# Attention on one core: maxima sent on ScalarE's queue, softmax sums inverted by way of DRAM and multiplied in on GpSimd

## What is computed

```
q_lat, kv_lat = h @ W_qd, h @ W_kvd          # h = rmsnorm(xn, w_ln1)
scores = einsum('bqhd,bkhd->bhqk', qq, kk) * scale      # 16 heads, 16 wide, causal
probs  = softmax(scores, axis=-1)
y      = einsum('bhqk,bkhd->bqhd', probs, v).reshape(B, S, H) @ W_o
x1     = xn + y
x2     = x1 + shared_expert(rmsnorm(x1)) + top2_of_7_experts(rmsnorm(x1))
```

## Time and profile before

| | |
|---|---|
| median of 3 runs | 4965.75 us |
| the profiled execution, its own time | 4929.39 us |
| its span | 4927.6 us |
| TensorE's mean granted clock in it | 0.889 of full speed |
| PE, VectorE, ScalarE, GpSimd busy | 79%, 68%, 48%, 44% of the span |

### The profile page before, as it was taken

One profiled execution on the slowest core, in us unless ns is written; L12 is line 12 of the kernel. 1 busy time (PEld: TensorE's weight loads), 2 busy tenths in 40 slices (PEclk: granted clock), 3 DMA queues, 4 the chain that ended last, 5 costly groups with the idle time before them and its releaser, 6 DMA issues.

```text
span 4927.6 us, 72057 instructions
## 1 busy us (share of the span) xinstructions
PE 3871.0 (79%) x22968; PEld 2870.5 (58%) x22968; DVE 3372.8 (68%) x5931; ACT 2389.0 (48%) x6217; POOL 2172.9 (44%) x1174
## 2 busy tenths in 40 slices
PE   3677777777777778599958888888888888888886
PEld 1333333334433344477747777777777777777776
DVE  2555555555555556222229999999999999999998
ACT  0322223222232333133337667767767767767764
POOL 3222222222222221100037777677677777777775
PEclk7888888888988989799978999999999999999998
DMA  4444434343433330476632212222222222122121
GB/s 70 64 66 66 65 61 67 58 66 61 66 61 61 63 59 31 122 211 211 210 99 76 76 71 80 78 73 76 78 73 78 75 79 80 68 82 77 71 76 41
DMA packets 285539, 399.85 MB, mean 81 GB/s; under 512 B 50773, under 2 KB 247766, under 8 KB 268824
## 3 DMA queue, kind: packets, MB, share of 16 engines
q1 hardware_dynamic: 272920, 362.63, 29.9%
q0 software_dynamic: 12288, 33.57, 2.0%
HBM read 313.26 MB, written 82.05 MB: 80 GB/s over the span
## 4 chain that ended last, share of the span: by engine, by line
DVE 19%; POOL 11%; PE 10%; issue 9%; DVEq 1%; ACT 1%; SPq 0%; POOLq 0%; DMA 0%; ACTq 0%
POOL m_ub L1505 9%; PE m_Y L1870 4%; DVE m_S L1723 4%; DVE m_S L1731 4%; DVE m_PR L1723 4%; DVE m_PR L1731 3%; PE m_Y L1880 3%; DVE m_sp_v L1700 2%; POOL m_yg L1515 1%; PE m_Y L1883 1%; DVE m_ub L1708 1%; POOL m_dtx L1484 1%; DVE m_yz L1742 1%; DVE m_st L1679 0%; PE m_F L1824 0%
## 5 line engine op out<-in xcount | busy, mean ns | idle before, releaser
L1505 POOL TENSOR_TENSOR m_ub<-m_Bb,m_dtx 128x2048 f32<-128x2048 f32 x256 | 1156.3, 4540 | 554.6 <-PE m_Y L1870 548.0
L1620 ACT ACTIVATE m_dA<-m_dt,m_a_neg 128x128 f32<-128x128 f32 x4096 | 1210.4, 392 | 29.6 <-DVE m_S L1731 25.6
L1870 PE MATMUL m_Y<-m_ub,m_ident 128*128 128x128 f32 x8192 | 1013.8, 288 | 240.2 <-DVE m_ub L1708 240.2
L1870 PEld LDWEIGHTS m_Y<-m_ub,m_ident 128*128 128x128 f32 x8192 | 995.3, 204 | 248.5 <-DVE m_ub L1708 247.7
L506 ACT ACTIVATE f_pt<-f_X 128x512 f32<-128x512 f32 (+1 forms) x704 | 378.4, 556 | 886.1 <-PE f_X L792 884.6
L559 DVE TENSOR_REDUCE f_nm<-f_Y 128x1 f32<-128x512 f32 (+3 forms) x896 | 430.3, 529 | 148.7 <-PE f_Y L786 147.0
L791 PE MATMUL f_X<-f_qst,f_kst 99*128 99x512 bf16 (+3 forms) x1024 | 300.1, 336 | 294.7 <-DMA f_qst<-f_nmT 213.0
L617 DVE RECIPROCAL f_O<-f_O 128x256 f32<-128x256 f32 x128 | 222.6, 1751 | 360.2 <-PE f_O L847 360.2
L1723 DVE SCALAR_TENSOR_TENSOR m_PR<-m_dA,m_S 128x512 f32<-128x512 f32 x512 | 355.5, 694 | 122.1 <-POOL m_ub L1505 50.0
L785 PE MATMUL f_Y<-f_kst,f_qst 96*128 96x512 bf16 (+3 forms) x1024 | 276.1, 324 | 161.1 <-DVE f_nm L559 128.2
L791 PEld LDWEIGHTS f_X<-f_qst,f_kst 99*128 99x128 bf16 x1024 | 108.9, 107 | 449.3 <-issue 310.0
(11 more groups left out here) (239 smaller groups left out, 6924.0 us busy)
## 6 DMA issues: line engine op xcount, KB each, us to landing
m_Bb<-m_bc_dram SPq DMA_DIRECT2D x64, 1024.0 KB, 4.7
m_Cb<-m_bc_dram SPq DMA_DIRECT2D x64, 1024.0 KB, 4.7
f_parts_dram<-f_parts SPq DMA_DIRECT2D x32, 768.0 KB, 4.5
f_kst<-f_parts_dram SPq DMA_DIRECT2D x192, 128.0 KB, 11.3
f_qst<-f_parts_dram SPq DMA_DIRECT2D x192, 128.0 KB, 12.3
e_rows<-sorted_rows SPq DMA_DIRECT2D x70, 256.0 KB, 2.7
e_wg<-Wg SPq DMA_DIRECT2D x70, 256.0 KB, 2.9
e_wu<-Wu SPq DMA_DIRECT2D x70, 256.0 KB, 3.9
```

The lines of the kernel that those rows point to most:

```text
L1505: pool.tensor_tensor(ub[:, h, i, :, :], Bb[:, s, :, :], dtx[:, par, m, None, s * SN:(s + 1) * SN].to_broadcast([P, NST, SN]), ALU.mult).th ...
L1620: last = act.activation(dA[:, h, i, n, :], dtt[:, par, m, s * SN:(s + 1) * SN], ACT.Exp, scale=a_neg[:, m, n:n + 1])
L1870: last = pe.matmul(Y[:, i * SN:(i + 1) * SN], ident[:, :], ub[:, h, i, n, :], start=False, stop=(n == NST - 1), skip_group_check=True)
```

## The change

The maxima are sent by ScalarE (`act.dma_start` in `nmt`) instead of SP. The sums are no longer spread by PE and inverted in full banks. For two groups at a time (a pair): `so` stores the four sum rows of both groups (4 partitions x 1024, 16 KB) to DRAM, `sl` loads them as a tile of 128x32, `rp` inverts that tile on VectorE, `ro` stores it, `rl` loads it back spread over 128 rows (128x1024, 512 KB, by a broadcast access pattern of 4 x 32 x 1024), and `ym` multiplies on GpSimd, 128x1024. All four are issued by ScalarE, and it waits before each of `so`, `sl`, `ro` and `rl` for what comes ahead. The second pair of a batch is finished in the next round (`sl1` to `ym1`). PE's wait before reusing a bank `f_O` is now for the copy. The second product of the shared expert is written over the first (`hm = sg`), and the table `AT` is new: 62 places rather than 74, `s1` over places 5 to 55 (before: 8 to 63), the group stores, `pfx`, `scat` and `nm` nearer to the round's end.

The diff (semaphores' declarations, the constant `f_sel` and line counts left out):

```diff
...
@@ -81,7 +80,11 @@
     rb = sb("f_rb", [P, 2, SEQ])
-    yT = sb("f_yT", [P, 4, SEQ])
+    yT = sb("f_yT", [P, NG, SEQ])
+    PAIRS = NG // 2
+    PW = HG * 2 * SEQ // P
+    sums = sb("f_sums", [P, PAIRS, PW])
+    shares = sb("f_shares", [P, 2, SEQ])
     parts = sb("f_parts", [P, PARTS, 4, SEQ], bf16)
@@ -119,7 +122,9 @@
     sg = sb("f_sg", [P, NS, SEQ])
-    hm = sb("f_hm", [P, NS, SEQ])
+    hm = sg
+    sums_dram = nc.dram_tensor("f_sums_dram", [PAIRS, HG, 2, SEQ], f32).ap()
+    shares_dram = nc.dram_tensor("f_shares_dram", [PAIRS, HG, 2, SEQ], f32).ap()
     parts_dram = nc.dram_tensor("f_parts_dram", [2, 8, HD, PARTS, 2, SEQ], bf16).ap()
@@ -131,40 +136,34 @@
         for n in range(N_S2[kb]):
-            if g > 0:
-                if kb == 1 and n == 0:
-                    S2_ITEMS.append(("bc", g - 1, 0))
-                if kb == 1 and n == 2:
-                    S2_ITEMS.append(("rc", g - 1, 0))
-                if kb == 2 and n == 0:
-                    S2_ITEMS.append(("rc", g - 1, 1))
-                if kb == 2 and n == 1:
-                    S2_ITEMS.append(("ym", g - 1, 0))
             S2_ITEMS.append(("s2", q, n))
...
                 S2_ITEMS.append(("pv", q - 1, 0))
-                if kb == 0:
+                if kb == 1 and g > 0:
                     S2_ITEMS.append(("oc", g - 1, 0))
...
     STAGE.update({kind: 1 for kind in ("s1", "nm", "nmt", "v")})
-    STAGE.update({kind: 0 for kind in ("xrload", "xn", "s2", "pv", "oc", "bc", "rc", "ym")})
-    STAGE.update({kind: -1 for kind in ("bc3", "rc3", "ym3", "wo", "h2", "ht", "route", "lg", "rank", "pfx", "scat", "g", "u", "d")})
+    STAGE.update({kind: 0 for kind in ("xrload", "xn", "s2", "pv", "oc", "so", "sl", "rp", "ro", "rl", "ym")})
+    STAGE.update({kind: -1 for kind in ("sl1", "rp1", "ro1", "rl1", "ym1", "wo", "h2", "ht", "route", "lg", "rank", "pfx", "scat", "g", "u", "d")})
     S1 = [("s1", i, n) for i in range(NH // 2) for n in range(3)]
-    AT = {0: [("xload", 0, 0)], 2: [("bc3", NG - 1, 0)], 3: [("rc3", NG - 1, 0)], 4: [("rc3", NG - 1, 1)], 6: [("ym3", NG - 1, 0)],
-          9: [("wo", 0, 0)], 12: [("xrload", 0, 0)], 16: [("h2", 0, 0)], 18: [("xn", 0, 0)], 20: [("ht", 0, 0)], 22: [("bn", 0, 0)],
-          25: [("route", 0, 0), ("lg", 0, 0)], 27: [("h1", 0, 0)], 30: [("rank", 0, 0)], 32: [("T", 0, 0)], 34: [("g", 0, 0)],
-          36: [("lat", 0, 0)], 38: [("u", 0, 0)], 40: [("kq", 0, 0)], 42: [("g", 1, 0)], 44: [("kq", 0, 1)], 46: [("u", 1, 0)],
-          47: [("split", 0, 0)], 49: [("pfx", 0, 0), ("scat", 0, 0)], 50: [("kq", 1, 0)], 53: [("d", 0, 0)], 54: [("kq", 1, 1)], 56: [("d", 1, 0)],
-          58: [("split", 1, 0)], 62: [("stack", 0, 0)], 66: [("nm", 0, 0)], 70: [("nmt", 0, 0)]}
+    AT = {0: [("xload", 0, 0)], 2: [("sl1", 1, 0)], 5: [("rp1", 1, 0)], 6: [("ro1", 1, 0)], 9: [("rl1", 1, 0)], 14: [("ym1", 1, 0)],
+          17: [("wo", 0, 0)], 19: [("xrload", 0, 0)], 23: [("h2", 0, 0)], 25: [("xn", 0, 0)], 27: [("ht", 0, 0), ("bn", 0, 0)],
+          31: [("route", 0, 0), ("lg", 0, 0)], 32: [("h1", 0, 0)], 35: [("rank", 0, 0), ("T", 0, 0)], 37: [("g", 0, 0)],
+          39: [("lat", 0, 0)], 40: [("u", 0, 0)], 42: [("kq", 0, 0)], 43: [("g", 1, 0)], 45: [("kq", 0, 1)], 46: [("u", 1, 0)],
+          48: [("split", 0, 0)], 49: [("kq", 1, 0)], 50: [("pfx", 0, 0), ("scat", 0, 0)], 52: [("d", 0, 0)], 53: [("kq", 1, 1)],
+          54: [("d", 1, 0)], 56: [("split", 1, 0)], 57: [("nm", 0, 0)], 59: [("nmt", 0, 0)], 60: [("stack", 0, 0)]}
     for n, item in enumerate(S1):
-        AT.setdefault(8 + n * 56 // len(S1), []).append(item)
+        AT.setdefault(5 + n * 51 // len(S1), []).append(item)
+    first_pair = S2_ITEMS.index(("oc", 1, 0)) + 1
+    for n, kind in ((0, "so"), (4, "sl"), (8, "rp"), (9, "ro"), (12, "rl"), (17, "ym")):
+        AT.setdefault(first_pair + n, []).append((kind, 0, 0))
     ORDER = []
...
     assert not AT
-    ORDER += [("pv", NG * TT - 1, 0), ("oc", NG - 1, 0), ("stack", 1, 0), ("v", 0, 0)]
+    ORDER += [("pv", NG * TT - 1, 0), ("oc", NG - 1, 0), ("so", 1, 0), ("stack", 1, 0), ("v", 0, 0)]
     FIRST, LAST = -2, BATCH
...
@@ -353,10 +355,6 @@
                 sp.dma_start(xr[:, :, :], src).then_inc(xr_loaded, 16)
-            if kind == "nmt":
-                held(*used(("nmt",), r))
-                for c in range(PARTS):
-                    sp.dma_start(qst[parity(kind, r)][KS + c:KS + c + 1, :, :], nmT[c * NH:(c + 1) * NH, :]).then_inc(nm_stacked, 16)
             if kind == "split":
...
@@ -472,6 +466,9 @@
                 tt(parts[:, 2, pair, :], kq_rest[:, pair, :], parts[:, 1, pair, :], ALU.subtract).then_inc(lo_ready[g], 1)
+            if kind in ("ym", "ym1"):
+                pool.wait_ge(shares_loaded, 16 * (PAIRS * b + i + 1))
+                tt(yT[:, 2 * i:2 * i + 2, :], yT[:, 2 * i:2 * i + 2, :], shares[:, :, :], ALU.mult).then_inc(y_done, 1)
             if kind == "wo":
...
@@ -505,6 +502,10 @@
+
+        def held(s, v):
+            act.wait_ge(s, v)
+            act.sem_inc(taken)
 
@@ -527,12 +528,29 @@
                 read(("nmt",), nmT[:, :], lambda bank: bank[0:PARTS * NH, 0:SEQ // 2].bitcast(bf16), ACT.Copy)
+                held(*used(("nmt",), r))
+                for c in range(PARTS):
+                    act.dma_start(qst[parity(kind, r)][KS + c:KS + c + 1, :, :], nmT[c * NH:(c + 1) * NH, :]).then_inc(nm_stacked, 16)
             if kind == "s2":
...
                 act.activation(yT[:, i, :], O[i % 2][:, :], ACT.Copy).then_inc(o_copied, 1)
+            if kind == "so":
+                held(o_copied, NG * b + 2 * i + 2)
+                act.dma_start(sums_dram[i, :, :, :], yT[HD:P:VA, 2 * i:2 * i + 2, :]).then_inc(sums_stored, 16)
+            if kind in ("sl", "sl1"):
+                held(sums_stored, 16 * (PAIRS * b + i + 1))
+                act.dma_start(sums[:, i, :], sums_dram[i, :, :, :].rearrange("j g t -> (j g t)").rearrange("(p c) -> p c", p=P)).then_inc(sums_loaded, 16)
+            if kind in ("ro", "ro1"):
+                held(shares_ready, PAIRS * b + i + 1)
+                act.dma_start(shares_dram[i, :, :, :].rearrange("j g t -> (j g t)").rearrange("(p c) -> p c", p=P), sums[:, i, :]).then_inc(shares_stored, 16)
+            if kind in ("rl", "rl1"):
+                held(shares_stored, 16 * (PAIRS * b + i + 1))
+                held(y_done, PAIRS * b + i)
+                act.dma_start(shares[:, :, :].rearrange("p g t -> p (g t)"),
+                              shares_dram[i, :, :, :].rearrange("j g t -> j (g t)")[:, None, :].to_broadcast([HG, VA, 2 * SEQ])).then_inc(shares_loaded, 16)
             if kind == "ht":
@@ -610,14 +628,9 @@
                 last.then_inc(xn_done, 1)
-            if kind in ("rc", "rc3"):
-
-                half = slice(j * SEQ // 2, (j + 1) * SEQ // 2)
-                dve.wait_ge(sums_spread, NG * b + i + 1)
-                dve.reciprocal(O[i % 2][:, half], O[i % 2][:, half]).then_inc(rec_done, 1)
-            if kind in ("ym", "ym3"):
-                dve.wait_ge(rec_done, 2 * (NG * b + i + 1))
-                dve.tensor_tensor(yT[:, i, :], yT[:, i, :], O[i % 2][:, :], ALU.mult).then_inc(y_done, 1)
+            if kind in ("rp", "rp1"):
+                dve.wait_ge(sums_loaded, 16 * (PAIRS * b + i + 1))
+                dve.reciprocal(sums[:, i, :], sums[:, i, :]).then_inc(shares_ready, 1)
             if kind == "nm":
@@ -700,13 +713,13 @@
             if kind == "g":
+                if i == 0 and (not isinstance(b, int) or b > 0):
+                    dve.wait_ge(*filled(("d", 1), before_(r)))
+                    dve.sem_inc(taken)
                 bank = full(("g", i), r)
...
             if kind == "u":
-                if i == 0 and (not isinstance(b, int) or b > 0):
-                    dve.wait_ge(*filled(("d", 1), before_(r)))
-                    dve.sem_inc(taken)
                 bank = full(("u", i), r)
@@ -798,7 +811,7 @@
                 if g >= 2 or not isinstance(b, int) or b > 0:
-                    pe.wait_ge(y_done, NG * b + g - 1)
+                    pe.wait_ge(o_copied, NG * b + g - 1)
             src = pt[:, PT_W:] if q % 2 else pt[:, 0:PT_W]
@@ -842,11 +855,8 @@
                 values(i, b, r)
-            if kind in ("bc", "bc3"):
-                pe.wait_ge(o_copied, NG * b + i + 1)
-                pe.matmul(O[i % 2][:, :], sel[:, :], yT[:, i, :], start=True, stop=True).then_inc(sums_spread, 1)
             if kind == "wo":
-                pe.wait_ge(y_done, NG * (b + 1))
+                pe.wait_ge(y_done, PAIRS * (b + 1))
                 for n in range(2):
...
                     for q in range(2):
```

More of the change, by code:

```diff
@@ L60, in build_attn @@
     rope = sb("f_rope", [P, 2, SEQ])
-    sel = sb("f_sel", [P, P])
     ident = sb("f_ident", [P, P])
@@ L243, in build_attn @@
     o_copied = sem("f_o_copied")
-    sums_spread = sem("f_sums_spread")
-    rec_done = sem("f_rec_done")
+    sums_stored = sem("f_sums_stored")
+    sums_loaded = sem("f_sums_loaded")
```

(8 more changed lines are left out.)

## The result

The changed kernel takes **5105.53 us** (median of 4 runs, 5100.71 to 5109.99) against 4975.34 for the kernel before in the same comparison (4965.02 to 4994.53): a ratio of **1.0257**, 95% interval 1.0218 to 1.0296, so slower. A repetition on another occasion gave 5097.24 and a ratio of 1.0207 (1.0185 to 1.0229). The forecast was 5032, 1.3% above 4965.75: the right sign, half the size, inside the range of 4895 to 5125.

The account below looks back on a forecast made before the run. Attention's rounds were bound by PE's wait for the maxima, sent behind the first group's loads. 60.8 us to `wo` plus 61.8 make 122.6 against 118.7; 15 rounds add 59, the tail 7: 4965.75 + 66, some 5032 us, range 4895 to 5125.

Parts of the forecast that it names:

- what is late next: At the first `s1` item: the first group's loads land at 41.6 us behind `pfx`, PE wants them at 30, waits 11.6.
- PE's stop at ScalarE's `split`: At the last scores behind `pfx`: PE gets there sooner, so its wait grows from 4.5 us to 9.
- Its inverses are ready early: Second pair's way: only an exponential behind the first `s1` item holds `ro`, which goes at 43.5 us and takes 4.5.
- the sum of 66: Whole kernel: 15 rounds, each 3.9 us longer, make 59 us, and the uncovered tail of the last round 7 more.
- The arrival of PE: PE reaches the first `s1` item at 30 us behind `pfx` and `wo` at 54, where it waits 6.8.
- From `wo` to the next `pfx`: Rest of the round: 63.2 us before, plus 4.6, less 2.6, 0.9 and 2.5, gives 61.8.
- the 2.5 us given back for the freed VectorE: Between `wo` and the next `pfx`: a third of PE's 7.5 us a round of waiting for VectorE's maxima goes.
- The broadcast: `rl`, 512 KB on ScalarE's queue: issued at 48 us, takes 10.4, lands at 58.4; GpSimd's product is ready at 60.8.
- rival 3: The broadcast runs on 4 engines, 9.4 us alone, landing near 62; a round 126.3 us, kernel 5092 us; chance 0.22.
- The queue: Maxima sent on ScalarE's own queue, nothing ahead: landing takes 4 us, between 2.1 and 12.4; the round begins at 27.

Follow-up runs that it names:

- The one part alone: The kernel before with only the sending of the maxima moved from SP to ScalarE, behind its copy: 4902.55 us, a ratio of 0.9944.

## Why the prediction was right and wrong

**Right: what is late next.** The first `s1` item was put at 41.6 us behind `pfx`, held by the first group's loads; it ran at 41.5. PE's stop at ScalarE's `split` was put at 9 us and measured at 9.2. The maxima's wait is gone from its place. `wo` waits for GpSimd's product, and the round is longer, as forecast.

**The step that failed** is the term "Its inverses are ready early" in the second pair's way. The prediction put the sums' store, their load and the inversion at nothing, gave no row for it, and took the exponential behind the first `s1` item as the only thing that holds `ro`. The runs show that the store took 8.1 us and the load 14.2, so that the inversion stood at 49.7. `ro` went at 50.2 instead of 43.5, 6.7 us later. Its landing took 6.4 us instead of the 4.5 that a small transfer in the traffic had been given, 1.9 more, and the broadcast went at 56.6 instead of 48. The broadcast took 9.3 us instead of 10.4, 1.1 less. Those are the whole 7.5 us by which `wo` came later (68.3 instead of 60.8), and 15 times 7.5, 113 us, are what the profiled executions have more than the sum of 66. Without the second pair's way a round is 112.5 us.

**The arrival of PE** was wrong in two places. At the first `s1` item it was put at 30, with a wait of 8 to 14 us for the loads. PE was there at 37.2 and waited 4.3. The round began at 31.0 instead of 27, at a granted clock of 0.50, and PE stood 2.9 us for ScalarE, which itself stood for the sums' store. This moved nothing, as the loads set that item. At `wo` PE was put at 54 and was there at 61.3, because VectorE stood before the inversion with the maxima queued behind it. That had no price of its own, as the inversion placed later shows. That PE's wait at `wo` was put at 6.8 us and measured at 7.1 is luck: both ends of it came 7 us late.

**From `wo` to the next `pfx`** 61.8 us were worked out and 61.9 measured, but the terms do not agree one by one. `wo` itself took 9.58 us instead of the 7.17 of before, since it starts at the lower clock. PE's waits for VectorE in this stretch are 6.2 us, and were 5.9 before, so the 2.5 us given back for the freed VectorE are not there. On the other side the clock was 1.00 from 1081 us on, where before it was 0.50 from 1016 to 1026. The inversions left out bound what freeing VectorE can bring: 0.4% of the kernel, about 1 us a round.

**The broadcast** was put at 10.4 us, the middle of two bounds; it took 9.3. It was the mechanism of rival 3 that made it so: four engines, with a share of 0.22 to 0.27 where nothing else runs, and 4.1 us once all sixteen take part. By the Trainium skill's rule ("DMA: Bandwidth & Descriptors", "Why a DMA increments its semaphore by 16 and not by 1") the outermost sizes 4 and 128 give four engines, and the trace agrees. The rival's bound for the broadcast alone, 9.4 us, was right. Its 5092 us lie nearest to the result, but by luck: it had the broadcast land at 62 after some 14 us beside the other loads, and it ran when they had ended and landed at 65.9, late because it was issued late.

**The queue.** 4 us were taken for the maxima from ScalarE's queue. Where they are sent ahead of the loads, 3.8 to 6.5 us are measured (the changed kernel with the broadcast in four, 500 to 1500 us). The one part alone shows that it was this being ahead, and not the queue: 9.4 us among the loads.

## What to carry to other kernels

Before a result is sent by way of DRAM, count the transfers that wait for each other and price each at what a small transfer takes in the traffic of that moment, here 3.6 to 14.2 us and not the 1.4 us of an empty machine; the engine that waits holds up all that stands behind it, but look for the end of the chain to see what is paid. A transfer that is late is helped first by moving what is ahead of it. In the kernel before, the first group's loads, sent 11 us behind `pfx` instead of 27 by one entry of a table, gave 4.35%, and another queue for the maxima 0.6%. Then look which transfer the traffic meets now: in the changed kernel the same move sped the sums' load up by 10.6 us and slowed the store behind it by 2.8. Give a broadcast from DRAM an outermost size that all sixteen engines can share.
